# The Gram stage of an attention kernel: q is multiplied with q and k at once, and only k is squared and summed

## The reference, cut to what matters

```
def _l2norm(x, eps=1e-12):
    nrm = jnp.sqrt(jnp.sum(x * x, axis=-1, keepdims=True))
    return x / jnp.maximum(nrm, eps)
q, k, v = jnp.split(qkv, 3, axis=1)
q = _l2norm(q.reshape(b, heads, cpg, hw))          # cpg = 48, hw = 16384
k = _l2norm(k.reshape(b, heads, cpg, hw))
attn = jnp.einsum('bhcn,bhdn->bhcd', q, k) * temperature
```

## Time and profile before

| | us |
|---|---|
| median of 3 runs | 6928.13 (6928.11 to 6961.05) |
| the profiled execution | 6940.06 |
| its span | 6938.5 |
| Gram stage, first load issued to the store of its result issued | 2319.25 to 2758.99 |
| PE busy over the whole span | 5361.6 (77%) |
| DVE busy over the whole span | 5420.2 (78%) |
| ACT busy over the whole span | 3091.4 (45%) |

### The profile page before, as it was taken

One profiled execution on the slowest core, in us unless ns is written; L12 is line 12 of the kernel. 1 busy time (PEld: TensorE's weight loads), 2 busy tenths in 40 slices (PEclk: granted clock), 3 DMA queues, 4 the chain that ended last, 5 costly groups with the idle time before them and its releaser, 6 DMA issues. The chain is left out here.

```text
span 6938.5 us, 79665 instructions
## 1 busy us (share of the span) xinstructions
PE 5361.6 (77%) x25018; PEld 2242.9 (32%) x25018; DVE 5420.2 (78%) x4182; ACT 3091.4 (45%) x3615; POOL 317.6 (5%) x492
## 2 busy tenths in 40 slices
PE   0999998999999576466665777769958887994887
PEld 0333333433333476233332222222212222221222
DVE  7223333999999799898995666669989996998998
ACT  0222222211111587255550000048857776885776
POOL 0111110000000000112120000000000000000000
PEclk9999999999999788678887787789978888997888
DMA  8666666999999996788887999946657764666775
GB/s 305 201 203 217 216 205 182 298 271 271 277 268 273 252 250 160 189 231 228 225 223 174 261 267 266 264 153 249 249 217 265 266 234 164 247 246 219 262 266 210
DMA packets 1173189, 1634.68 MB, mean 236 GB/s; under 512 B 82996, under 2 KB 903925, under 8 KB 1143285
## 3 DMA queue, kind: packets, MB, share of 16 engines
q1 hardware_dynamic: 834805, 1352.75, 63.6%
q10 hardware_dynamic: 314880, 201.39, 10.3%
q0 software_dynamic: 23424, 79.66, 4.5%
HBM read 975.88 MB, written 657.67 MB: 235 GB/s over the span
## 5 line engine op out<-in xcount | busy, mean ns | idle before, releaser
L544 PE MATMUL dw_p<-dw_it,dw_tt 128*128 128x512 f32 x2304 | 1027.8, 607 | 114.5 <-DVE dw_tt L460 81.5
L583 DVE SCALAR_TENSOR_TENSOR dw_vo<-dw_vi,keep_wv,dw_vo 128x2048 f32<-128x2048 f32 x384 | 903.1, 2352 | 13.6
L909 PE MATMUL bc_p<-bc_z,bc_wc 128*32 128x256 f32 x9216 | 571.3, 413 | 350.6 <-DVE bc_z L951 350.6
L951 DVE STREAM_TRANSPOSE bc_z<-bc_xp 96x1536 f32<-96x1536 f32 (+1 forms) x256 | 718.3, 2912 | 98.1 <-DMA bc_xp<-d 95.1
L1160 PE MATMUL ap_p<-ap_vt,ap_pw 96*96 96x512 f32 x1024 | 588.5, 740 | 190.2 <-DMA ap_xt<-in_x 185.3
L345 PE MATMUL pw_p<-pw_xh,pw_wlo 128*128 128x512 f32 x1280 | 586.2, 605 | 185.1 <-POOL pw_xh L298 185.1
L544 PEld LDWEIGHTS dw_p<-dw_it,dw_tt 128*128 128x128 f32 x2304 | 442.5, 194 | 699.9 <-issue 667.3
L561 ACT ACTIVATE dw_ot<-dw_p 128x512 f32<-128x512 f32 x384 | 216.4, 599 | 925.7 <-PE dw_p L544 661.1
L909 PEld LDWEIGHTS bc_p<-bc_z,bc_wc 128*32 128x32 f32 x9216 | 322.5, 119 | 599.5 <-issue 436.2
L1537 DVE TENSOR_TENSOR_SCAN wb_sums<-wb_ewt,wb_fb 128x3078 f32<-128x3078 f32 x64 | 424.3, 6630 | 2.3
L1797 DVE TENSOR_TENSOR_SCAN wf_sums<-wf_ewt,wf_fb 128x3078 f32<-128x3078 f32 x64 | 424.3, 6630 | 2.3
(11 more groups left out here) (323 smaller groups left out, 9145.3 us busy)
## 6 DMA issues: line engine op xcount, KB each, us to landing
u<-pw_ut SPq DMA_DIRECT2D x64, 2048.0 KB, 8.2
dw_it<-u SPq DMA_DIRECT2D x192, 512.0 KB, 10.9
d<-dw_ot ACTq DMA_DIRECT2D x192, 512.0 KB, 12.3
gr_qk<-d SPq DMA_DIRECT2D x128, 768.0 KB, 9.2
bb_d<-wb_bb SPq DMA_DIRECT2D x64, 1536.0 KB, 5.2
wf_bb<-bb_d SPq DMA_DIRECT2D x64, 1536.0 KB, 7.5
bc_xp<-d SPq DMA_DIRECT2D x216, 288.0 KB, 10.1
bc_xp<-d POOLq DMA_DIRECT2D x192, 288.0 KB, 9.2
```

The source lines that it names most:

```text
L544: mm = nc.tensor.matmul(po[c][:, :].rearrange("p (b w) -> p b w", b=B), tt[:, h, 3 * c + dx, 0:H], it[:, h, B * c:B * (c + 1), dx:dx + W], ...
L583: nc.vector.scalar_tensor_tensor(vo[:, h], src, w, vo[:, h], ALU.mult, ALU.add).then_inc(tapped, 1)
L909: mm = nc.tensor.matmul(po[q % NBANK][32 * c4:32 * c4 + 32, :, :], wc[:, c, dx, :, :].rearrange("p j r -> p (j r)"), z[:, h, c, :, dx:dx + ...
L951: last = nc.vector.transpose(z[rows, h, :, b % 2, 1 + S * k:1 + S * k + S], xp[rows, b % 2, k, :, :].rearrange("p s c -> p c s"))
```

## The change

Each Gram matmul keeps its 48 q columns as weights, and now moves all 96 channels, q and k, past them. The PSUM tile gets 96 columns: q with q in the first 48, q with k in the next. The diagonal of q with q is the sum of squares of q, so that only k is squared and summed: NE falls from 4 to 2. `finish` is split into `keep` (the copy, now 48x96) and `roots` (one item later), `score` into `diagonal` (adds the partial sums, masks with the identity, sums each row) and a shorter `score` (one item later). PE now waits for `summed` of item n - 3 ahead of its matmuls, and for `rooted` only ahead of the small matmul. Cut to its core:

```
-    NE = QK // E
+    NE = CPG // E
-        ss = st.sb("ss", [128, NB, QK])
+        ss = st.sb("ss", [128, NB, CPG])
-        pg = [st.ps(f"p{h}", [128, CPG]) for h in range(NB)]
-        pn = [st.ps(f"n{h}", [CPG, QK]) for h in range(NB)]
+        pg = [st.ps(f"p{h}", [128, QK]) for h in range(NB)]
+        pn = [st.ps(f"n{h}", [CPG, CPG]) for h in range(NB)]
...
-                pe.wait_ge(scored, n + 1)
-                pe.wait_ge(rooted, n + 1)
+                pe.wait_ge(summed, n + 1)
                 for w in range(W):
                     p = 64 * (w % 2)
-                    mm = nc.tensor.matmul(pg[h][p:p + CPG, :], qk[:, h, 0:CPG, w], qk[:, h, CPG:QK, w],
+                    mm = nc.tensor.matmul(pg[h][p:p + CPG, :], qk[:, h, 0:CPG, w], qk[:, h, :, w],
                                           start=w < 2, stop=w >= W - 2, skip_group_check=True)
                 mm.then_inc(product, 1)
+                pe.wait_ge(rooted, n + 1)
                 pe.wait_ge(reduced, NE * (n + 1))
...
+            def keep(n):
+                h = n % NB
+                act.wait_ge(product, n + 1)
+                act.wait_ge(summed, n + 1)
+                nc.scalar.activation(gb[:, h, :], pg[h][64:64 + CPG, :], ACT.Copy).then_inc(copied, 1)
+            def roots(n):
+                h = n % NB
+                act.wait_ge(normed, n + 1)
+                wait(act, scored, n - NB + 1)
+                nc.scalar.activation(nrm[:, h, 0:CPG], pn[h][:, :], ACT.Sqrt)
+                act.wait_ge(diag, n + 1)
+                nc.scalar.activation(nrm[:, h, CPG:CPG + 1], nq[:, h:h + 1], ACT.Sqrt).then_inc(rooted, 1)
...
-                                         qk[:, h, E * e:E * e + E, :].rearrange("p c w -> p (c w)"), ACT.Square).then_inc(squared, 1)
+                                         qk[:, h, CPG + E * e:CPG + E * e + E, :].rearrange("p c w -> p (c w)"), ACT.Square).then_inc(squared, 1)
                 if n:
-                    finish(n - 1)
+                    keep(n - 1)
+                if n > 1:
+                    roots(n - 2)
...
+            def diagonal(n):
+                h = n % NB
+                dve.wait_ge(copied, n + 1)
+                wait(dve, scored, n - NB + 1)
+                nc.vector.tensor_tensor(ga[:, h, :], pg[h][0:CPG, :], gb[:, h, :], ALU.add).then_inc(summed, 1)
+                dve.wait_ge(summed, NB + n + 1)
+                wait(dve, diag, n)
+                nc.vector.tensor_tensor(nqd[:, :], ga[:, h, 0:CPG], ident[:, :], ALU.mult).then_inc(masked, 1)
+                dve.wait_ge(masked, n + 1)
+                nc.vector.tensor_reduce(nq[:, h:h + 1], nqd[:, :], AX.X, ALU.add).then_inc(diag, 1)
...
             for n in range(NI):
                 reduce(n)
                 if n:
-                    score(n - 1)
+                    diagonal(n - 1)
+                if n > 1:
+                    score(n - 2)
```

More of the change, by code:

```diff
@@ L610, in gram_scores @@
         temp = st.sb("temp", [CPG, HEADS])
-        gb = st.sb("gb", [CPG, NB, CPG])
-        ga = st.sb("ga", [CPG, CPG])
-        nrm = st.sb("nrm", [CPG, NB, QK])
+        gb = st.sb("gb", [CPG, NB, QK])
+        ga = st.sb("ga", [CPG, NB, QK])
+        nrm = st.sb("nrm", [CPG, NB, CPG + 1])
         nqd = st.sb("nqd", [CPG, CPG])
-        nq = st.sb("nq", [CPG, 1])
+        nq = st.sb("nq", [CPG, NB])
         a = st.sb("a", [CPG, NI, CPG])
-        pg = [st.ps(f"p{h}", [128, CPG]) for h in range(NB)]
-        pn = [st.ps(f"n{h}", [CPG, QK]) for h in range(NB)]
+        pg = [st.ps(f"p{h}", [128, QK]) for h in range(NB)]
+        pn = [st.ps(f"n{h}", [CPG, CPG]) for h in range(NB)]
         loaded = [st.sem(f"loaded{h}") for h in range(NB)]
-        consts, vectors, product, normed, squared, reduced, copied, rooted, scored, small, stored = map(
-            st.sem, ("consts", "vectors", "product", "normed", "squared", "reduced", "copied", "rooted", "scored", "small",
-                     "stored"))
+        consts, vectors, product, normed, squared, reduced, copied, summed, masked, diag, rooted, scored, small, stored = map(
+            st.sem, ("consts", "vectors", "product", "normed", "squared", "reduced", "copied", "summed", "masked", "diag", "rooted",
+                     "scored", "small", "stored"))
         block = st.block()
@@ L638, in _ @@
                                      img[:, c0 + e:c0 + e + 12, :]).then_inc(loaded[n % NB], 16)
-            sp.wait_ge(scored, NI + NB)
+            sp.wait_ge(scored, NI)
             sp.dma_start(attn_d.rearrange("(n c) k -> c n k", c=CPG), a[:, :, :]).then_inc(stored, 16)
@@ L674, in _ @@
             act.sem_inc(rooted, NB)
-            def finish(n):
+            def keep(n):
                 h = n % NB
                 act.wait_ge(product, n + 1)
-                wait(act, scored, n + 1)
+                act.wait_ge(summed, n + 1)
                 nc.scalar.activation(gb[:, h, :], pg[h][64:64 + CPG, :], ACT.Copy).then_inc(copied, 1)
+            def roots(n):
+                h = n % NB
                 act.wait_ge(normed, n + 1)
-                nc.scalar.activation(nrm[:, h, :], pn[h][:, :], ACT.Sqrt).then_inc(rooted, 1)
+                wait(act, scored, n - NB + 1)
+                nc.scalar.activation(nrm[:, h, 0:CPG], pn[h][:, :], ACT.Sqrt)
+                act.wait_ge(diag, n + 1)
+                nc.scalar.activation(nrm[:, h, CPG:CPG + 1], nq[:, h:h + 1], ACT.Sqrt).then_inc(rooted, 1)
             for n in range(NI):
@@ L689, in _ @@
                     nc.scalar.activation(sq[:, e % 2, :, :].rearrange("p c w -> p (c w)"),
-                                         qk[:, h, E * e:E * e + E, :].rearrange("p c w -> p (c w)"), ACT.Square).then_inc(squared, 1)
+                                         qk[:, h, CPG + E * e:CPG + E * e + E, :].rearrange("p c w -> p (c w)"), ACT.Square).then_inc(squared, 1)
                 if n:
-                    finish(n - 1)
-            finish(NI - 1)
+                    keep(n - 1)
+                if n > 1:
+                    roots(n - 2)
+            keep(NI - 1)
+            roots(NI - 2)
+            roots(NI - 1)
         @block.vector
         def _(dve):
-            dve.sem_inc(scored, NB)
+            dve.sem_inc(summed, NB)
             dve.wait_ge(consts, 3)
@@ L710, in score @@
                 nc.vector.tensor_scalar(nrm[:, h, :], nrm[:, h, :], 1e-12, None, ALU.max).then_inc(small, 1)
[L711 to L724, removed]
+                dve.wait_ge(small, 3 * n + 1)
+                nc.vector.reciprocal(nrm[:, h, :], nrm[:, h, :]).then_inc(small, 1)
+                dve.wait_ge(small, 3 * n + 2)
+                nc.vector.scalar_tensor_tensor(a[:, n, :], ga[:, h, CPG:QK], nrm[:, h, CPG:CPG + 1], nrm[:, h, 0:CPG], ALU.mult,
+                                               ALU.mult).then_inc(small, 1)
+                dve.wait_ge(small, 3 * n + 3)
                 nc.vector.tensor_scalar(a[:, n, :], a[:, n, :], temp[:, hd:hd + 1], None, ALU.mult).then_inc(scored, 1)
@@ L729, in _ @@
                 if n:
-                    score(n - 1)
+                    diagonal(n - 1)
+                if n > 1:
+                    score(n - 2)
+            diagonal(NI - 1)
+            score(NI - 2)
             score(NI - 1)
```

## The result

| | before | after |
|---|---|---|
| median, us | 6941.24 (6928.11 to 6961.05, 4 runs) | 7050.18 (7047.60 to 7052.38, 4 runs) |
| ratio | | 1.0154, 95% interval 1.0123 to 1.0186 |
| profiled execution, us | 6940.06 | 7052.38 |
| Gram stage, us | 439.7 | 555.0 |

A forecast was written before the change was run, and what follows sets the result against it. The Gram stage was taken as a chain on PE: 24.25 + 16 T + 5.3 + 4.5 = 34 + 16 T, with T = 30 514 us against 439.7, 74 us longer. Median forecast 7002 us, range 6860 to 7100.

The forecast's parts named there:

- T: Length of an item's run of Gram matmuls on PE: 18.86 us before, 30.0 forecast, break-even at 25.35.
- reads shared alike: Gram matmuls: weights and moving reads counted alike, 96 becoming 144, so a run takes 1.5 x 18.86 = 28.3 us.
- the calmest run doubled: Gram matmuls: the fastest run before, 16.26 us, doubles with the moving columns to 32.5 us.
- The lone moving stream: Gram matmuls: strided moving columns alone set a run, 128 pairs x 96 x 2.08 ns = 25.6 us.
- which slow PE from 18 to 13 or 14 instructions per us: Gram runs: ACT and DVE slow PE's matmuls, and would have half their long work; used in choosing 30.0 us.
- 5.3 us for small matmuls and restarts between runs: Seams between PE's Gram runs: this time, 408.55 less 301.7 and 101.5, stays as before.
- The end: From the last Gram run's end to the store: 6.94 us before, 4.5 forecast without the wait for the last reduction.
- Waits to about 0: Small matmul L665 on PE: its waits for DVE's reductions go from 104.6 us to about 0.
- The signs named ahead: Gram stage: L665's wait near zero, PE busy near 485 us, runs about 30, 8 or 9 instructions per us, load gaps.
- Rival 1: Gram stage: columns cheap, runs at most 20.5 us, loads become the bound, 65 us less, 6863; chance 0.20.
- Rival 2: Gram stage: gain and loss cancel, runs between 23.2 and 27.5 us, time 6932; chance 0.18.
- Rival 3: Gram stage: everything doubles, the slow pace too, runs of 37.7 us, time 7126; chance 0.14 with above.

The follow-up runs named there:

- Experiment 6: Changed kernel with the weights as 48 pixels side by side of one channel, moving operand still 512 bytes apart, diagonal squared; 6959.3 us in a single run.
- experiment 7: Changed kernel with all 128 matmuls of an item into one column tile, partitions 0 to 47; 7278.7 us in a single run.
- experiment 2: Kernel before with ACT squaring and DVE summing only one channel of each piece of 24; 6870.8 us against 6931.7.
- experiment 1: Changed kernel with ACT squaring and DVE summing only one channel of each piece of 24; 7051.4 us in one run.
- Experiment 8: Kernel before with 96 moving columns as the only part of the change, all four squares and reductions kept; 7049.6 us in one run.
- experiments 3 and 4: Channels 132 floats apart (528 bytes) in place of 128, in the changed kernel and in the kernel before; single runs 6883.9 and 6857.7 us against 6931.7.

## Why the prediction was right, and where its sizes were off

The direction, the mechanism and the place were right: 7002 forecast and 6860 to 7100 given, 7050 measured; the wait for DVE went from 104.6 to 0.0, PE became the bound, the runs grew by more than the waits had been. That the figure came so near is in part luck: of the arguments for T = 30.0 one was wrong and another didn't hold as it was read, as the list says.

- **The term that was mis-sized is T:** 30.0 taken, 32.9 measured. 16 x 2.9 is 47 us, more than the whole miss of 41 us between 514 and 555 for the stage. I took the middle between reads shared alike (28.3) and the calmest run doubled (32.5), and the doubled calm run was the nearer. (The middle of the two is 30.4, not 30.0, which would have added 6 us.) That doubling fits isn't a rule either: T goes from 18.9 to 32.9 with the columns, 1.75 times.
- The lone moving stream, 2.08 ns per column from the shortest Gram matmul, gave 25.6 us. Experiment 6, in which the weights' step is out of the way, measured 27.2, but the nearness is in part chance. By experiment 7 a lone stream takes at most 184 ns, 1.92 ns per column, and would give at most 23.6 us, below the break-even at 25.35. What I left out are two things that make up the difference to 32.9: the moving streams of the two tiles slow each other (27.2 against 23.6), and the weights' strided reads come on top, 5.7 us a run, though they are loaded beside the moving columns.
- ACT and DVE, "which slow PE from 18 to 13 or 14 instructions per us", was wrong. Without their long work both the slow and the fast pace remain (experiment 2), and T = 32.9 stays to the tenth (experiment 1). The fast pace was read in a window without loads, but loads don't decide it either: the run of 16.26 us from 2510.88 had them at 290 GB/s all along. The starving works one way, from PE to ACT and DVE.
- 5.3 us for small matmuls and restarts between runs: they vanished into the runs, 16 runs of 32.94 fill the 527.1 us from the first matmul to the last. The end took 3.4 us (2871.07 to 2874.46), 4.5 had been taken.
- Waits to about 0, loads covered by the runs, small work unimportant: all as forecast. That two reductions fit beside a run was argued with 16.8 and 10 us; they take 5.7 each. Experiment 8 adds that all four would have fitted, so that half of the change had no part in the result.
- The signs named ahead were there: the wait of L665 at 0.0, 8 instructions per us at either clock, squares and reductions well above 2.76 and 3.32 us, and windows without loads. PE's busy time in the stage, near 485 forecast, was 527.1, which is the miss in T again.
- Rival 1, cheap columns and a stage bound by loads, was told as a cost of starting instructions. The cause is another one, the step in memory, but its end was real: at a step of 528 bytes the changed kernel has T = 22.5 and is 1% faster than before. On the recorded step it was out, as the row of 266 ns against 246 had said.
- Rival 2, gain and loss that cancel, stood on the lone stream's 25.6 and on matmuls that run freely once half of the long work is gone. Both failed, as above: T = 32.9 with all of that work left out too.
- Rival 3, T = 37.7, fell because the slow pace of 48 columns has no double: the slowest run took 20.64 us, and 96 columns take 32.9 always, not 41.
- The Trainium skill (SBUF — State Buffer, section "Door 1: The DMA port swizzle") says that each access that crosses to a new 16-byte line pays a penalty. The case agrees in so far as the moving operand side by side gives 15.6. But a step of 528 bytes crosses a line at every element as one of 512 does, and T is 22.5 there against 32.9, so that rule doesn't tell these 10.4 us.
- The Trainium skill (SBUF — State Buffer, section "Who interferes with whom") says that PE and ACT never wait on anyone. By that, experiments 3 and 4 would have left the squares as they were, but they went from 5.9 and 5.7 to 2.8 us.

## What to carry to other kernels

Before work is moved from one engine to another, ask what it costs there per element as this kernel reads it, and look at the shortest instruction of the same access rather than at one of the same shape: 266 ns for 48 strided columns beside 246 for 96 contiguous ones gave the direction, though not the size: 2.08 ns per column was read from it, and experiment 7 allows at most 1.92. Where an engine is slower than its own shortest duration, find out what slows it before taking work off it; here four floats of padding per channel, 4.6 KB per partition for the three buffers, took the stage from 439.7 to 362.6 us, and no engine got work for it. When a pace doesn't follow the clock, the step in memory is a cheap thing to vary early.

## What the runs showed of the hardware that was not expected

- Matmul operands read with a step of 512 bytes are slow with nothing long beside them (experiment 1): a run of 256 instructions of 96 columns takes 32.9 us at 512 bytes, 24.2 at 520, 22.5 at 528, 22.3 at 576, and 15.6 with the moving operand contiguous and the weights still at 512.
- Two column tiles reading weights and moving columns at 512 bytes slow a plain, contiguous ACT square from 2.77 to 5.9 us and a DVE reduction from 3.35 to 5.7 us, at 48 columns at times to 17.5 and 16.8. With one tile at its slower pace, or with one of the two operands contiguous, or at 520, 528 and 576 bytes, they don't.
- One tile with both operands at 512 bytes takes 184 ns per instruction of 96 columns. Two tiles take 129, and 106 with the weights side by side, where two independent tiles would take 92 at most (184 / 2).
- At 48 columns and 512 bytes PE's pace moves, between runs (16 to 20 us) and within one (28 to 40 instructions in 2 us at one clock), with or without work and loads beside it. At 96 columns and 512 bytes, and at 48 with 528 bytes, it is steady: 32.9 to 33.4 us and 11.8 to 12.1. What moves it was not found; it may be why the kernel before spreads over 34 us in its runs (6929.73 to 6963.84) and the changed one over 5, but that wasn't tested.
